# The way into a state space mixer by stages, with part of its work moved into the scan

## What is computed

```python
xz = einsum('btd,ed->bte', x, in_proj_w); x_in, z = xz[..., :Dd], xz[..., Dd:]
x_c = conv_general_dilated(swapaxes(x_in, 1, 2), conv_w, padding=[(D_CONV - 1, 0)], feature_group_count=Dd) + conv_b
x_conv = silu(swapaxes(x_c, 1, 2))
ssm_params = einsum('btd,ed->bte', x_conv, x_proj_w)      # B: 16 rows, C: 16 rows, dt: 1 row
dt = softplus(ssm_params[..., -1:] * dt_proj_w[None, None, :, 0] + dt_proj_b)
h = exp(dt * A) * h + dt * B * x_conv                     # over 512 tokens, for each of 16 states
y = sum over states of h * C;  y = y * silu(z);  out = y @ out_proj_w.T
```

## Time and profile before

| | |
|---|---|
| runs, median of 3 | 1152.23 us (1150.41 to 1152.46) |
| profiled execution, its own time | 1153.68 us |
| its span, first to last instruction | 1151.9 us |
| busy share of the span | PE 88%, DVE 55%, ACT 47%, POOL 17% |
| mean granted clock of TensorE | 0.953 of 2.4 GHz |

### The profile page before, as it was taken

The page is one execution under the profiler, slowest core; times in us unless marked ns, Lnnn a source line. Parts: engine busy times, 40 slices in busy tenths (PEclk is TensorE's granted clock), DMA queues, the critical chain, the costliest instruction groups (busy, mean ns, idle before and its releaser), DMA issues.

```text
span 1151.9 us, 11536 instructions
## 1 busy us (share of the span) xinstructions
PE 1012.3 (88%) x3673; PEld 439.1 (38%) x3700; DVE 629.3 (55%) x1175; ACT 538.7 (47%) x979; POOL 193.6 (17%) x173
## 2 busy tenths in 40 slices
PE   4799999998799999999769968677777999999896
PEld 2345544454222222233235643222223444444343
DVE  2222323334888868775253435589995554545564
ACT  3232232233367667676533434665664324464540
POOL 9100000000000000000574540076661000000000
PEclk9799999999899999999979988989999899999998
DMA  8620000030021202100003425000000211110032
GB/s 176 202 85 0 1 1 1 15 75 0 22 70 43 69 23 70 43 22 2 24 21 92 117 82 151 0 1 1 0 1 0 91 48 47 47 45 19 6 105 73
DMA packets 66588, 54.41 MB, mean 47 GB/s; under 512 B 18440, under 2 KB 58397, under 8 KB 66436
## 3 DMA queue, kind: packets, MB, share of 16 engines
q1 hardware_dynamic: 64228, 50.96, 15.7%
q0 software_dynamic: 2304, 2.76, 0.8%
HBM read 41.65 MB, written 13.77 MB: 48 GB/s over the span
## 4 chain that ended last, share of the span: by engine, by line
PE 68%; DVE 13%; ACT 8%; issue 7%; DMA 2%; POOL 1%; SPq 1%; another core or an unknown queue 1%; DVEq 0%; ACTq 0%; POOLq 0%
PE psum L675 65%; ACT sb_scr L1556 5%; DVE sb_scr L2201 3%; DVE sb_scr L2528 2%; DVE sb_scr L2537 2%; ACT psum L1556 1%; PE psum L832 1%; PE psum L1248 1%; DVE sb_scr L2076 0%; ACT sb_qstack L1556 0%; POOL expert_in L636 0%; DVE sb_x L2052 0%; DMA sb_scr<-pick_rows 0%; DVE sb_scr L2074 0%
## 5 line engine op out<-in xcount | busy, mean ns | idle before, releaser
L1556 ACT ACTIVATE sb_scr<-psum 128x512 f32<-128x512 f32 (+4 forms) x644 | 320.6, 537 | 369.0 <-PE psum L675 301.5
L675 PE MATMUL psum<-sb_h,sb_wide 128*128 128x512 f32 x448 | 210.6, 600 | 0.8 <-ACT sb_scr L1556 0.8
L2201 DVE TENSOR_REDUCE sb_scr<-psum 128x2 f32<-128x1024 f32 x128 | 154.8, 1222 | 46.4 <-PE psum L675 45.8
L675 PE MATMUL psum<-sb_scr,sb_wide 128*128 128x512 f32 x256 | 127.7, 600 | 0.3 <-DVE sb_scr L2578 0.3
L675 PEld LDWEIGHTS psum<-sb_h,sb_wide 128*128 128x128 f32 x448 | 83.7, 193 | 93.6 <-issue 91.9
L675 PE MATMUL psum<-sb_kstack,sb_qstack 96*128 96x512 bf16 x256 | 98.3, 395 | 11.3 <-DVE sb_scr L2201 8.5
L2140 DVE TENSOR_SCALAR sb_scr<-psum,sb_b 128x512 f32<-128x512 f32 x48 | 34.6, 747 | 126.3 <-PE psum L675 126.3
L658 POOL TENSOR_TENSOR sb_scr<-sb_scr 128x512 f32<-128x512 f32 x64 | 80.9, 1267 | 104.2 <-ACT sb_scr L1556 104.1
L1556 ACT ACTIVATE sb_scr<-psum,sb_b 128x512 f32<-128x512 f32 x48 | 31.2, 685 | 137.4 <-PE psum L675 137.4
L675 PE MATMUL psum<-sb_qstack,sb_kstack 128*128 128x512 bf16 x233 | 90.7, 395 | 4.4 <-ACT sb_scr L1556 3.2
L2568 DVE TENSOR_TENSOR sb_scr<-psum,sb_scr 128x512 f32<-128x512 f32 x64 | 44.1, 689 | 81.7 <-ACT sb_scr L1556 81.7
(11 more groups left out here) (255 smaller groups left out, 1306.2 us busy)
## 6 DMA issues: line engine op xcount, KB each, us to landing
sb_scr<-weight_rows SPq DMA_DIRECT2D x32, 256.0 KB
sb_qstack<-q_bounce SPq DMA_DIRECT2D x48, 96.0 KB
sb_kstack<-k_bounce SPq DMA_DIRECT2D x144, 32.0 KB
sb_scr<-pick_rows SPq DMA_DIRECT2D x8, 512.0 KB
expert_in<-sb_scr SPq DMA_DIRECT2D x4, 645.0 KB, 6.6
sb_scr<-expert_in SPq DMA_DIRECT2D x8, 322.5 KB
...
```

Source lines behind the costliest of these rows:

```text
L675: return nc.tensor.matmul(out_, w, r, start=start, stop=stop, **kw)
L1556: return nc.scalar.activation(out_, in_, func, **kw)
L2201: v.reduce_max(headmax[:, g % 2, t:t + 2, j], banks, AX.X).then_inc(sem("maxed"), 1)
```

## The change

All norms of the sublayer come first, in a hand-written order in which PE turns, centres and squares between them. `xpad` goes: the convolution and the first projection become one, four matmuls of `h`, shifted, with `wconv`, which is the projection's matrix times the tap's weight for each channel. PE (one matmul with ones, `conv_spread`) and DVE (one product) make `wconv` before the routed rows arrive. The four batches' convolutions go to banks 4, 5, 0 and 1. ACT has the log and exp table for the norms, then that of silu, then the first again. `dtv` and the 32 state rows (`bc_raw`) are copied out of PSUM by ACT; DVE reads them from SBUF. Only batch 0's parts, softplus and dtx are made before the scan; those of batches 1 to 3 stand inside it. `dtv`, `dtl`, `xconv` and `bc_raw` move to the space of `qstack` and `kstack`, which the second mixer no longer uses.

Lines taken out are not repeated below; they stand in the functions above. In short:

```diff
             for b in range(NB):
+                pool.wait_ge(sem("dtx_ready"), b + 1)
...
+            mm(bank(0), ones[:], conv_diag[:].rearrange("p k d -> p (k d)")).then_inc(sem("conv_spread"), 1)
...
+            def center2(b):
+                pe.wait_ge(x_ready, N2LN + b + 1)
                 if b >= 2:
+                    pe.wait_ge(ln_done, N2LN + b - 1)
+                mm(bank(b % 2), center[:], x[:, b, :]).then_inc(sem("ln_centered"), 1)
+            def variance2(b):
+                pe.wait_ge(sem("ln_squared"), N2LN + b + 1)
+                mm(bank(6 + b % 2), mean[:], squares[:, b % 2, :]).then_inc(sem("ln_var"), 1)
+            def project_z(b):
+                pe.wait_ge(ln_done, N2LN + b + 1)
+                if b >= 2:
+                    pe.wait_ge(sem("zgate_ready"), b - 1)
+                mm(bank(2 + b % 2), wT[:, WZ2, :], h[:, b, :]).then_inc(sem("z_done"), 1)
+            def convolve(b, begin=0, end=DCONV):
+                pe.wait_ge(ln_done, N2LN + b + 1)
+                for back in range(begin, end):
+                    m = mm(psum[:, (4, 5, 0, 1)[b], back:S], wconv[:, DCONV - 1 - back, :], h[:, b, 0:S - back],
+                           back == 0, back == DCONV - 1, skip_group_check=True)
+                if end == DCONV:
+                    m.then_inc(sem("conv_ready"), 1)
...
+                if b == 0:
+                    pe.wait_ge(ln_done, N2LN + NB)
+                if b >= 2:
+                    pe.wait_ge(sem("dtv_ready"), 2 * (b - 1))
+                at = (6, 4)[b % 2]
+                mm(bank(at), dt_rep[:], xconv[:, b, :])
+                mm(bank(at + 1), wT[:, WSSM, :], xconv[:, b, :]).then_inc(sem("ssm_done"), 1)
             turn_back(0)
+            pe.wait_ge(setup, SETUP.index("wconv") + 1)
+            center2(0)
+            turn_back(1)
+            variance2(0)
+            center2(1)
+            turn_back(2)
+            variance2(1)
+            project_z(0)
+            center2(2)
+            convolve(0, 0, 2)
+            turn_back(3)
+            variance2(2)
+            convolve(0, 2)
+            center2(3)
+            project_z(1)
+            variance2(3)
+            convolve(1)
+            convolve(2)
+            project_z(2)
+            state_inputs(0)
+            convolve(3)
+            project_z(3)
+            for b in range(1, NB):
+                state_inputs(b)
+            pe.wait_ge(sem("dtv_ready"), 2 * NB)
+            pe.wait_ge(sem("zgate_ready"), NB)
...
             def spread_b(i):
                 b, n = divmod(i, NSTATE)
+                if n == 0:
+                    pe.wait_ge(sem("bc_parts"), b + 1)
...
+            def gate_silu(b):
+                act.wait_ge(sem("z_done"), b + 1)
+                f(zgate[:, b, :], bank(2 + b % 2), ACT.Silu).then_inc(sem("zgate_ready"), 1)
+            def deviation2(b):
+                n = NB * ATTN2 + b + 1
+                act.wait_ge(sem("ln_var"), n)
+                f(rstd[:, b, :], bank(6 + b % 2), ACT.Ln, bias=eps[:]).then_inc(sem("ln_logged"), 1)
+                act.wait_ge(sem("ln_logged"), n)
+                f(rstd[:, b, :], rstd[:, b, :], ACT.Exp, scale=-0.5).then_inc(sem("ln_rstd"), 1)
...
+                act.wait_ge(sem("dtv_ready"), 2 * b + 1)
+                f(dtl[:, b, :], dtv[:, b, :], ACT.Abs).then_inc(sem("dtl_step"), 1)
+                act.wait_ge(sem("dtl_step"), n + 1)
+                f(dtl[:, b, :], dtl[:, b, :], ACT.Exp, scale=-1.0).then_inc(sem("dtl_step"), 1)
+                act.wait_ge(sem("dtl_step"), n + 2)
+                f(dtl[:, b, :], dtl[:, b, :], ACT.Ln, bias=one[:]).then_inc(sem("dtl_step"), 1)
...
+            for b in range(NB):
+                square(NB * ATTN2, b, 2)
+                deviation2(b)
+            nc.scalar.preload_act_table_set("silu_and_others")
+            def take_state_inputs(b):
+                at = (6, 4)[b % 2]
+                act.wait_ge(sem("ssm_done"), b + 1)
+                f(dtv[:, b, :], bank(at), ACT.Identity, bias=dt_b[:], scale=dt_w[:]).then_inc(sem("dtv_ready"), 1)
+                f(bc_raw[:, b, :], psum[0:2 * NSTATE, at + 1, :], ACT.Copy).then_inc(sem("dtv_ready"), 1)
+            for b in range(NB):
+                conv_silu(b)
+                gate_silu(b)
+                if b == NB - 2:
+                    take_state_inputs(0)
             nc.scalar.preload_act_table_set(LOG_EXP)
+            softplus(0)
+            for b in range(1, NB):
+                take_state_inputs(b)
...
+                if i in (2, 5, 8):
+                    softplus(i // 3 + 1)
...
+            dve.wait_ge(sem("conv_spread"), 1)
+            v.tensor_tensor(wconv[:], bank(0).rearrange("p (k d) -> p k d", k=DCONV),
+                            wT[:, WX2, :].unsqueeze(1).broadcast_to([P, DCONV, D]), ALU.mult).then_inc(setup, 1)
...
             def state_inputs(b):
+                dve.wait_ge(sem("dtv_ready"), 2 * b + 2)
...
+            def normalize2(b):
+                dve.wait_ge(sem("ln_rstd"), NB * ATTN2 + b + 1)
+                v.tensor_tensor(h[:, b, :], bank(b % 2), rstd[:, b, :], ALU.mult).then_inc(ln_done, 1)
+            def steps_taken(b):
+                dve.wait_ge(sem("dtl_step"), 3 * b + 3)
+                dve.wait_ge(sem("dtv_ready"), 2 * b + 1)
+                v.scalar_tensor_tensor(dt[:, b, :], dtv[:, b, :], 0.0, dtl[:, b, :], ALU.max,
+                                       ALU.add).then_inc(sem("dt_ready"), 1)
+                dve.wait_ge(sem("dt_ready"), b + 1)
+                v.tensor_tensor(dtx[:, b, :], dt[:, b, :], xconv[:, b, :], ALU.mult).then_inc(sem("dtx_ready"), 1)
...
             combine(0)
             add_routed(0)
...
+            combine(1)
+            add_routed(1)
+            combine(2)
+            normalize2(0)
+            add_routed(2)
+            combine(3)
+            normalize2(1)
+            add_routed(3)
+            normalize2(2)
+            normalize2(3)
+            state_inputs(0)
+            steps_taken(0)
...
+                if i in (2, 4, 6):
+                    state_inputs(i // 2)
+                if i in (8, 10, 12):
+                    steps_taken(i // 2 - 3)
```

More of the change, by code:

```diff
@@ L153, in build @@
         kstack = sb("kstack", [P, HEADS, S], BF16)
-        xpad = sb("xpad", [P, NB, DCONV - 1 + S])
+        wconv = sb("wconv", [P, DCONV, D])
         conv_diag = sb("conv_diag", [P, DCONV, P])
@@ L287, in build @@
         dt, dtx, zgate = (batches(NB * S * n) for n in range(3))
-        xconv, dtl, dtv = batches(6144), batches(10240), batches(12288)
         RB, RC, RD = 4, 2, 2
@@ L1808, in softplus @@
             def softplus(b):
                 n = 3 * b
-                for i in range(2):
-                    act.wait_ge(sem("dtv_ready"), b + i + 1)
-                    f(dtl[:, b + i, :], dtv[:, b + i, :], ACT.Abs).then_inc(sem("dtl_step"), 1)
-                for i in range(2):
-                    act.wait_ge(sem("dtl_step"), n + i + 1)
-                    f(dtl[:, b + i, :], dtl[:, b + i, :], ACT.Exp, scale=-1.0).then_inc(sem("dtl_step"), 1)
-                for i in range(2):
-                    act.wait_ge(sem("dtl_step"), n + 2 + i + 1)
-                    f(dtl[:, b + i, :], dtl[:, b + i, :], ACT.Ln, bias=one[:]).then_inc(sem("dtl_step"), 1)
@@ L1821, in _ @@
-            for b in range(NB + 1):
-                if b < NB:
-                    square(NB * ATTN2, b, 2)
-                if b >= 1:
-                    act.wait_ge(sem("proj2_done"), b)
-                    f(xpad[:, b - 1, DCONV - 1:], bank((b - 1) % 2), ACT.Copy).then_inc(sem("xin_ready"), 1)
-                    f(zgate[:, b - 1, :], bank(2 + (b - 1) % 2), ACT.Silu).then_inc(sem("zgate_ready"), 1)
-                    conv_silu(b - 1)
-                if b < NB:
-                    nc.scalar.preload_act_table_set(LOG_EXP)
-                    deviation(NB * ATTN2, b)
-                if b == NB - 1:
-                    softplus(0)
+                act.wait_ge(sem("dtv_ready"), 2 * b + 1)
```

74 lines of the change are left out of this document (13 added, 61 removed).

## The result

The changed kernel takes 1154.84 us (median of 15 runs, 1152.32 to 1158.11) against 1152.23 (15 runs, 1147.15 to 1155.85): the ratio is 1.0028, interval 1.0015 to 1.0041, so it is slower by 1.7 to 4.7 us. The profiled execution took 1154.13 with a span of 1152.3.

A forecast was written before the change was run, and what follows sets the result against it. No engine is full in the way in, so a chain through several bounds it; DVE bounds the scan. -15.1 + 20.9 + 0.5 = +6.3 us takes the profiled 1153.68 to 1160.0, median 1158.5; alone 1155.5 to 1161, range with rivals 1146.5 to 1162.

The forecast's parts named there:

- the mechanism that was named: In the scan, DVE instructions reading only SBUF wait for a whole POOL product, so the inserted work costs more.
- the waiting: Time the DVE work inserted in the scan waits for POOL: 11.4 of 23.2 us.
- Way in: Into the third mixer, up to its first scan: scan at 735.8 instead of 750.93, 15.1 us earlier (13.5 to 16).
- Table loads: ACT's loads in the way into the mixer: 1.28 us each, nothing added for the skill's drain of 1380 ns.
- Insertions: DVE's parts in states 2, 4, 6 and steps in 8, 10, 12: 23.2 us, fourteenth scan 20.9 later after the first.
- my sign: In the scan: prediction wrong if DVE's meetings with POOL are absent or last less than a whole product.
- softplus work beside the scan: ACT's softplus, 1.9 us each, lies beside the inserted DVE work; a decay is wanted 0.2 to 1 us after it is made.
- Sum: Whole kernel: -15.1 for the way in, +20.9 for the scan, +0.5 for PE's clock, +6.3 us.
- Rival 1: In the scan POOL doesn't meet DVE: inserted work 11.8, sum -5.1, 1147.1 us, faster; chance 0.26.
- Rival 2: In the scan only POOL's drive under way blocks DVE: inserted work 17.05 us, 1152.3, no change; chance 0.16.
- Rival 3: PE stays at low clock; four states behind the last inserted work cost 0.7 more each, 2.8 not 0.5: 1160.8; chance 0.08.
- Rival 4: Way in gains less: ACT's copies and last inputs end 2 us later, 1160.5; chance 0.50 together with the forecast.

The follow-up runs named there:

- e1: Changed kernel with each instruction inserted in the scan taking one input from PSUM instead of SBUF, values not the model's: 1152.66 us against 1153.47 before the change.
- e2: Changed kernel without parts, dt and dtx of batches 1 to 3, whose states use batch 0's: ratio 0.9918 to the kernel before.
- e9: As e2, the same work left out, but ACT makes softplus one pass a state in states 1 to 9: ratio 0.9925 to the kernel before.

## Why the prediction was right, and where its terms were off

Slower was forecast, with a chance of 0.61, and slower it is, by the mechanism that was named. The size was about half of the forecast's: 2.6 by the medians and 1.7 to 4.7 by the interval, against 6.3. The 1154.84 lies in the range of 1146.5 to 1162, but 0.7 below the 1155.5 at which I had the forecast without its rivals begin. The direction did not hang on luck: the forecast turns to faster when the waiting totals under 5.1, and it was 8.5.

- **Way in.** Forecast 15.1 less, measured 14.2. The order of events is the one walked through: PE's run without a wait from 710.58, ACT's last copy ends at 732.97 (forecast 733.0), first scan at 735.74 (735.8). The times agree to 0.1 although the expert rows came 1.0 earlier, so the walk was 0.9 too short, 0.7 of it between them and PE's run (forecast 710.9, 20.25 behind the rows; measured 20.93). The added product for wconv stayed hidden: DVE still waits 2.93 for the gather behind it.
- **Table loads.** The function behind each load begins as it ends (712.15 + 1.28, then 713.44; 725.10 + 1.28, then 726.39). No further time, as the earlier trace rows had it, against the drain of about 1.38 us that the Trainium skill gives in "ScalarE: Activation LUTs", What ACT_TABLE_LOAD costs; the measurement decides.
- **Insertions.** The mechanism was right: e1 takes the meeting away and 4.8 of the 17.4 go; e2 takes the insertions away and 12.05 go. The size was off. From the end of a read to the next scan the six took 3.5, 4.4, 4.5, 2.55, 3.1 and 2.2, 20.2 together, where I had 4.9, 4.7, 4.7, 2.15, 3.4 and 3.4, 23.2. The mis-sized term is the waiting, 11.4 forecast and 8.5 measured. I took one of POOL's products to be under way at the start of every insertion, from the phase of the steady scan, and then, but for state 8, a second one of 1.27: eleven waits, where nine came. In the trace one is well under way at the start in states 4 and 10 only; elsewhere PE's spread and ACT's copy had come later, the first instruction went through (0.40, 0.68), and the product that began during it was met next. No wait reached 1.27, since POOL's product starts ahead of the instruction that it holds (0.25 in the first meeting of state 4) and that instruction ends behind the product by less than its own length (0.27 of 0.41). By the letter of my sign, "last less than a whole product", this was a miss; what holds is that each instruction ended behind the end of a product. I had 1.27 from the 1.97 of 582.88, read as a wait for one product alone; POOL's copy ahead of that product (582.44, 0.63) was still under way when DVE's instruction began. To the fourteenth scan that is 42.46, where 45.9 was forecast.
- **What hides what.** I called softplus work beside the scan, at no cost. e2 and e9 show a cost, which the insertions cover. The forecast was not hurt by it, but the expectation of e2 was, by 5.
- **Sum.** -14.2 + 17.4 + 0.1 = +3.3 by the spans up to the last scan, and +1.7 to +4.7 by the runs; forecast +6.3. Two of the terms were too large, 0.9 and 3.5, with opposite signs.
- **Rivals.** Rival 1, no meeting: refuted by the rows and by e1, which is that kernel on the chip and came out at or just below before, not 5 below, in part since reading PSUM makes its casts longer (2.8). Rival 2, only the product under way blocks: seven of the nine meetings were with a product that began during the insertion (749.62 above), so as a mechanism it is refuted; but its total of 17.05 is as far from 20.2 as mine. Rival 3, cold clock behind the insertions: from the fourteenth scan on the states take 97.52 against 97.40, so 0.1, not 2.8. Rival 4: 0.9 in place of 2.

The rule of the Trainium skill that I weighed ("SBUF — State Buffer", Who interferes with whom) holds in the rows read here: instructions with two SBUF inputs are held, and those with one in PSUM are not (e1). It says that copies and casts can be held too, in a two-port mode; with the 32-row casts free, as I read it then, the sum would have been 2 lower. Here they were held (1.29, 1.24, 1.37), when they read SBUF.

Open: the 1.0 to 2 us by which the spans behind the scan differ between kernels of the same code there; and what the half clock alone costs or saves within the insertions.
